# LSTM gates kept in PSUM, and five slots for gathered rows, in a graph network's LSTM

## What is computed

```python
seq = x[col].reshape(n, deg, d)            # 6250 nodes, 17 steps, 128
def step(carry, x_t):
    h, c = carry
    gates = x_t @ w_ih.T + h @ w_hh.T + b
    i, f, g, o = jnp.split(gates, 4, axis=-1)
    c = sigmoid(f) * c + sigmoid(i) * tanh(g)
    h = sigmoid(o) * tanh(c)
    return ((h, c), None)
```

## Time and profile before

| | us |
|---|---|
| median of 3 runs (2754.47 to 2767.64) | 2761.33 |
| the profiled execution | 2727.64 |
| its span | 2725.8 |

### The profile page before, as it was taken

One profiled execution on the slowest core, in us unless ns is written; L12 is line 12 of the kernel. 1 busy time (PEld: TensorE's weight loads), 2 busy tenths in 40 slices (PEclk: granted clock), 3 DMA queues, 4 the chain that ended last, 5 costly groups with the idle time before them and its releaser, 6 DMA issues. The chain is left out here.

```text
span 2725.8 us, 31186 instructions
## 1 busy us (share of the span) xinstructions
PE 2091.4 (77%) x10250; PEld 1626.9 (60%) x10250; DVE 1669.4 (61%) x4013; ACT 1030.3 (38%) x2257; POOL 1805.5 (66%) x1672
## 2 busy tenths in 40 slices
PE   6588888888888888888677677766776676767866
PEld 5477777767677777777545455544554444544545
DVE  4455655655566666665657556665675665656767
ACT  3455555555555555555422222222222222222321
POOL 1667777677777777775366667766777677767660
PEclk8789989989999989998878779877888788878889
DMA  8666766566666666665211111111111111111111
GB/s 303 203 188 205 209 184 183 165 179 178 179 182 178 180 177 182 177 177 145 85 43 42 47 47 44 47 42 43 47 50 44 42 46 47 46 43 45 40 42 48
DMA packets 120893, 310.32 MB, mean 114 GB/s; under 512 B 29042, under 2 KB 42460, under 8 KB 120604
## 3 DMA queue, kind: packets, MB, share of 16 engines
q0 software_dynamic: 93264, 273.00, 35.5%
q1 hardware_dynamic: 27468, 35.33, 3.8%
HBM read 288.95 MB, written 19.26 MB: 113 GB/s over the span
## 5 line engine op out<-in xcount | busy, mean ns | idle before, releaser
L645 POOL DMA_INDIRECT sender<-table,src_index x832 | 899.3, 1081 | 444.7 <-issue 285.1
L372 POOL DMA_INDIRECT shared<-gates,seq_index x833 | 895.2, 1075 | 383.3 <-issue 236.2
L426 ACT ACTIVATE shared<-bank,bias 128x512 f32<-128x512 f32 (+1 forms) x884 | 556.1, 664 | 583.7 <-PE bank L402 236.2
L694 PE MATMUL bank<-msg,select 128*128 128x256 f32 x1664 | 500.3, 452 | 277.0 <-DVE msg L789 165.6
L390 PE MATMUL bank<-ident,shared 128*128 128x128 f32 x3332 | 467.2, 293 | 181.4 <-issue 78.4
L694 PEld LDWEIGHTS bank<-msg,select 128*128 128x128 f32 x1664 | 353.2, 223 | 365.0 <-issue 299.0
L390 PEld LDWEIGHTS bank<-ident,shared 128*128 128x128 f32 x3332 | 412.1, 151 | 244.4 <-issue 199.5
L720 ACT ACTIVATE h<-bank,b 128x512 f32<-128x512 f32 x104 | 71.5, 688 | 861.6 <-remote 456.5
L763 DVE TENSOR_TENSOR select<-shared,rel 128x512 f32<-128x512 f32 x208 | 142.3, 684 | 390.6 <-remote 358.8
L402 PE MATMUL bank<-h_hi,w_lo 128*128 128x512 f32 (+1 forms) x832 | 353.1, 424 | 7.4 <-issue 7.0
L681 PEld LDWEIGHTS bank<-a,h 64*128 64x128 f32 x1664 | 217.8, 196 | 209.7 <-issue 204.6
(11 more groups left out here) (90 smaller groups left out, 2037.3 us busy)
## 6 DMA issues: line engine op xcount, KB each, us to landing
shared<-gates,seq_index POOLq DMA_INDIRECT x833
sender<-table,src_index POOLq DMA_INDIRECT x832
gates<-shared SPq DMA_DIRECT2D x49, 256.0 KB, 3.9
feats<-attr_in SPq DMA_DIRECT2D x13, 256.0 KB
x<-x_nodes_in SPq DMA_DIRECT2D x12, 256.0 KB
table<-up SPq DMA_DIRECT2D x12, 256.0 KB, 2.3
out<-x SPq DMA_DIRECT2D x12, 256.0 KB
shared<-x_t_in SPq DMA_DIRECT2D x3, 704.0 KB, 9.7
```

Source lines behind the costliest of these rows:

```text
L372: pool.indirect_dma_start(out=rows[:, k % 4, j, :], out_offset=None, in_=t["gates"], in_offset=bass.IndirectOffsetOnAxis(ap=seq_index[:, c ...
L426: act_e.activation(act[:, k % 2, gate, 0:width], banks[n % 8][:, 0:width], ACT.Tanh if gate == 2 else ACT.Sigmoid, bias=bias2[:, gate:gate ...
L645: pool.indirect_dma_start(out=sender[:, hg % 4, j, :], out_offset=None, in_=t["table"], in_offset=bass.IndirectOffsetOnAxis(ap=src_index[: ...
L694: last = pe.matmul(acc_bank[i % 3][:, 0:MSG], select[:, hg % 2, j, :], msg[:, hg % 2, j].rearrange("p k u -> p (k u)"), start=(tile in FIR ...
```

## The change

ScalarE writes gates i, f and o back into the banks that it reads them from; the candidate g alone goes to SBUF, into `candidate`, two buffers of 512 columns. VectorE's product of i and candidate goes into `candidate`, forget gate by cell and the hidden product are written into their own banks, and the high and low parts of h are taken from the bank of gate o. Tanh of the cell of item k-1 comes ahead of gate f of item k and waits for the hidden product of k-3 instead of the low part. ScalarE's waits for the cell and the low part, and VectorE's last wait of an item, are gone. TensorE waits bank by bank: gate i's for the input product (the cell in step 0) of k-2, gate f's for its cell, gate o's for its low part of h. The rows have five slots. The first block's views of the pool move, with the same sizes.

```diff
-        pool_cols = 4 * 4 * 4 * HID + 8 * CHUNK
+        slot_cols = 4 * 4 * HID
+        pool_cols = SLOTS * slot_cols + 2 * CHUNK
...
                     for k, (step, c) in enumerate(WORK):
-                        if 4 <= k < NCH + 4:
-                            pool.wait_ge(s_gate, 4 * (k - 3))
-                        elif k >= 4:
-                            pool.wait_ge(s_turned, k - 3 - NCH)
+                        if SLOTS <= k < NCH + SLOTS:
+                            pool.wait_ge(s_gate, 4 * (k - SLOTS + 1))
+                        elif k >= SLOTS:
+                            pool.wait_ge(s_turned, k - SLOTS + 1 - NCH)
...
-                        if k >= 2:
-                            pe.wait_ge(s_act, 4 * (k - 1))
                         for q, gate in enumerate(GATES):
                             bank, cols = banks[4 * (k % 2) + q], slice(gate * HID, (gate + 1) * HID)
+                            if k >= 2 and q == 0:
+                                if k - 2 < NCH:
+                                    pe.wait_ge(s_cell, k - 1)
+                                else:
+                                    pe.wait_ge(s_ig, k - 1 - NCH)
+                            if k >= 2 and q == 2:
+                                if k - 2 < NCH:
+                                    pe.wait_ge(s_act, 4 * (k - 2) + 3)
+                                else:
+                                    pe.wait_ge(s_cell, k - 1)
+                            if k >= 2 and q == 3:
+                                pe.wait_ge(s_hidden, k - 1)
...
-                            act_e.wait_ge(s_hidden, k - 1)
+                            act_e.wait_ge(s_new, k - 1)
                         act_e.activation(tanh_c[:, k % 2, 0:width], cell[:, c0:c0 + width],
...
-                            if q == 0 and k >= 2:
-                                act_e.wait_ge(s_cell, k - 1)
-                            if q == 3 and k >= 2:
-                                act_e.wait_ge(s_hidden, k - 1)
+                            if q == 2 and k:
+                                tanh_cell(k - 1)
+                            values = banks[n % 8][:, 0:width]
                             act_e.wait_ge(s_gate, n + 1)
-                            act_e.activation(act[:, k % 2, gate, 0:width], banks[n % 8][:, 0:width],
+                            act_e.activation(candidate[:, k % 2, 0:width] if gate == 2 else values, values,
...
-                        if k:
-                            tanh_cell(k - 1)
...
-                        dve.tensor_tensor(o, o, tanh_c[:, k % 2, 0:width], ALU.mult).then_inc(s_new, 1)
+                        dve.tensor_tensor(out, out, tanh_c[:, k % 2, 0:CHUNKS[WORK[k][1]][1]], ALU.mult).then_inc(s_new, 1)
...
-                        dve.tensor_copy(h_hi[:, c0:c0 + width], act[:, k % 2, 3, 0:width]).then_inc(s_hi, 1)
+                        dve.tensor_copy(h_hi[:, c0:c0 + width], banks[4 * (k % 2) + 3][:, 0:width]).then_inc(s_hi, 1)
...
-                        dve.tensor_tensor(h_lo[:, c0:c0 + width], act[:, k % 2, 3, 0:width],
+                        dve.tensor_tensor(h_lo[:, c0:c0 + width], banks[4 * (k % 2) + 3][:, 0:width],
                                           h_hi[:, c0:c0 + width].bitcast(F32), ALU.subtract).then_inc(s_hidden, 1)
...
-                            dve.tensor_tensor(gates[:, 0], gates[:, 0], gates[:, 2], ALU.mult).then_inc(s_ig, 1)
+                            dve.tensor_tensor(added, put, added, ALU.mult).then_inc(s_ig, 1)
...
-                            dve.tensor_tensor(gates[:, 1], gates[:, 1], here, ALU.mult).then_inc(s_fc, 1)
+                            dve.tensor_tensor(keep, keep, here, ALU.mult).then_inc(s_fc, 1)
...
-                            dve.tensor_tensor(here, gates[:, 0], gates[:, 1], ALU.add).then_inc(s_cell, 1)
+                            dve.tensor_tensor(here, keep, added, ALU.add).then_inc(s_cell, 1)
...
-                        dve.wait_ge(s_act, 4 * k + 4)
```

More of the change, by code:

```diff
@@ L32 @@
 GATES = (0, 2, 1, 3)
+SLOTS = 5
 GROUP = 8
@@ L118, in build @@
         s_const = sem("s_const")
-        s_wait = [sem(f"s_gather{i}") for i in range(4)]
+        s_wait = [sem(f"s_gather{i}") for i in range(SLOTS)]
         def flat_view(tile):
@@ L177, in build @@
             pool_of = shared[:, NODE_COLS:NODE_COLS + pool_cols]
-            rows_cols = 4 * 4 * 4 * HID
-            rows = pool_of[:, 0:rows_cols].rearrange("p (s j n) -> p s j n", s=4, j=4)
-            act = pool_of[:, rows_cols:rows_cols + 8 * CHUNK].rearrange("p (s g n) -> p s g n", s=2, g=4)
+            rows = pool_of[:, 0:SLOTS * slot_cols].rearrange("p (s j n) -> p s j n", s=SLOTS, j=4)
+            candidate = pool_of[:, SLOTS * slot_cols:pool_cols].rearrange("p (s n) -> p s n", s=2)
             x_t = cell
-            in_rows = rows.rearrange("p s j n -> p (s j) n")
-            w_ih = act[:, 0, 0, :]
-            inside, inside2 = (act[:, 1].rearrange("p g n -> p (g n)")[:, i:i + EDGE_TILES] for i in (0, 1024))
+            in_rows = pool_of[:, 0:8 * CHUNK].rearrange("p (s n) -> p s n", s=8)
+            w_ih, inside, inside2 = (pool_of[:, (8 + i) * CHUNK:(8 + i) * CHUNK + cols]
+                                     for i, cols in ((0, CHUNK), (1, EDGE_TILES), (3, EDGE_TILES)))
             seq_index = sb("seq_index", [P, NODE_TILES * STEPS], I32, scope=scope)
@@ L372, in _ @@
                             pool.indirect_dma_start(
-                                out=rows[:, k % 4, j, :], out_offset=None, in_=t["gates"],
+                                out=rows[:, k % SLOTS, j, :], out_offset=None, in_=t["gates"],
                                 in_offset=bass.IndirectOffsetOnAxis(ap=seq_index[:, col:col + 1], axis=0),
-                            ).then_inc(s_wait[k % 4], 16)
+                            ).then_inc(s_wait[k % SLOTS], 16)
                 @block.tensor
                 def _(pe):
-                    landed = [0] * 4
+                    landed = [0] * SLOTS
                     pe.wait_ge(s_idx, 64)
@@ L382, in _ @@
                         c0, width = CHUNKS[c]
-                        landed[k % 4] += 16 * (width // P)
-                        pe.wait_ge(s_wait[k % 4], landed[k % 4])
-                        if k >= 2:
-                            pe.wait_ge(s_act, 4 * (k - 1))
+                        landed[k % SLOTS] += 16 * (width // P)
+                        pe.wait_ge(s_wait[k % SLOTS], landed[k % SLOTS])
                         for q, gate in enumerate(GATES):
                             bank, cols = banks[4 * (k % 2) + q], slice(gate * HID, (gate + 1) * HID)
+                            if k >= 2 and q == 0:
[10 more added lines that the diff above has]
+                                pe.wait_ge(s_hidden, k - 1)
                             for j in range(width // P):
-                                last = pe.matmul(bank[:, j * P:(j + 1) * P], rows[:, k % 4, j, cols], ident[:],
+                                last = pe.matmul(bank[:, j * P:(j + 1) * P], rows[:, k % SLOTS, j, cols], ident[:],
                                                  is_transpose=True, start=(j == 0), stop=False,
@@ L437, in hidden_product @@
                     def hidden_product(k):
-                        width = CHUNKS[WORK[k][1]][1]
+                        out = banks[4 * (k % 2) + 3][:, 0:CHUNKS[WORK[k][1]][1]]
                         dve.wait_ge(s_tanh, k + 1)
-                        o = act[:, k % 2, 3, 0:width]
-                        dve.tensor_tensor(o, o, tanh_c[:, k % 2, 0:width], ALU.mult).then_inc(s_new, 1)
+                        dve.tensor_tensor(out, out, tanh_c[:, k % 2, 0:CHUNKS[WORK[k][1]][1]], ALU.mult).then_inc(s_new, 1)
                     def hidden_hi(k):
@@ L459, in _ @@
                         here = cell[:, c0:c0 + width]
-                        gates = act[:, k % 2, :, 0:width]
+                        put, keep = banks[4 * (k % 2)][:, 0:width], banks[4 * (k % 2) + 2][:, 0:width]
+                        added = candidate[:, k % 2, 0:width]
                         n = k - NCH + 1
@@ L463, in _ @@
                         if step == 0:
-                            dve.tensor_tensor(here, gates[:, 0], gates[:, 2], ALU.mult).then_inc(s_cell, 1)
+                            dve.tensor_tensor(here, put, added, ALU.mult).then_inc(s_cell, 1)
                         else:
-                            dve.tensor_tensor(gates[:, 0], gates[:, 0], gates[:, 2], ALU.mult).then_inc(s_ig, 1)
+                            dve.tensor_tensor(added, put, added, ALU.mult).then_inc(s_ig, 1)
                         if k:
```

## The result

| | before, us | after, us |
|---|---|---|
| median (4 runs each) | 2757.9 | 2928.6 |
| lowest to highest | 2752.34 to 2767.64 | 2920.24 to 2933.78 |
| profiled execution | 2727.64 | 2933.78 |
| mean granted TensorE clock in it | 0.861 | 0.884 |

After takes 1.0612 times as long as before [1.0569, 1.0655]: 171 us more by the medians. The forecast was 303 us more.

What follows compares the result with a forecast made beforehand. GpSimd's gathers were taken to fill 67.7 of 72.6 us an LSTM step. Hold 172 + clock 70 + slow instructions 60 - step 0's 3 = +299 us on 2727.6: 3027, or 3064 at the median; range 2910 to 3190.

Steps and rivals of the forecast that it cites:

- The hold of gate o's bank: LSTM steps 1 to 16: TensorE waits at gate o for h_lo of k-2; 6.70 us a chunk against 4.50, +172 us.
- The chain: LSTM, gate g's matmuls, tanh g, VectorE's operations up to h_lo, then TensorE's last transposes: 6.70 us between first matmuls.
- The clock: TensorE in LSTM steps 1 to 16: granted clock 0.88, 24% of the time at the lower level, +70 us (0 to +110).
- Slow instructions: TensorE in LSTM steps 1 to 16: before's stalls ahead of transposes, 68.5 us, stay; +60 us (0 to +110).
- the ring: LSTM steps 1 to 16: the round through TensorE, ScalarE and VectorE that sets the chunk period, 6.70 us at full clock.
- Step 0: First LSTM step, no matmuls: a gather a slot earlier and 0.1 us shorter, 70.4 to about 67, -3 us (-9 to +3).
- PSUM operands: LSTM, VectorE and ScalarE: PSUM forms take the SBUF forms' times, pitch 0.60 us, only h_hi's pitch rising from 0.47.
- Tanh moved ahead: ScalarE in the LSTM: taking tanh of the cell ahead of sigmoid f is worth nothing in steps 1 to 16.
- Five slots: LSTM gathers: a fifth slot lets a gather be issued a chunk earlier, worth nothing in steps 1 to 16.
- Rival 1: LSTM steps 1 to 16: gathers were the bound and the hold is hidden; -102 us, 2659 us, chance 6%.
- Rival 3: TensorE in the LSTM: regular standing keeps it at the lower clock, 8.5 us a chunk; +500 us, 3260 us, chance 9%.
- the other 16 us: Each LSTM step of before beyond TensorE's 56.2 us: gathers not landed, stretches at half clock, TensorE's instructions coming slowly.

Runs made afterwards that it cites:

- e1: After with VectorE finishing product, high and low part of item k-1 before item k, and ScalarE's cell tanh ahead of gate i: 2720.25 us, 1.0009 of before.
- e2: After with the hidden product in an SBUF tile, TensorE's gate-o wait ending with that product: 2729.33 us, 1.0046 of before.
- e3: Before with one added wait, TensorE for the low part of k-2 ahead of gate o's transposes of k: 3215.7 us.
- e8: After with tanh of the cell of k-1 behind gate o of k, as in before: 3313.26 us.
- e7: After with four slots instead of five: 2899.82 us, 1.0649 of before.
- e5: Before with each gather replaced by a plain DMA of the same 256 KB from SyncE, rows side by side, GpSimd silent: 2414.87 us.
- e6: Before with gathers for even items only from step 1 on: 2459.68 us.

## Why the prediction was right, and where its sizes were off

The direction, the cause and the place were right, and the time lay in the range, near its lower end: of the 303 us forecast 171 came, because two terms that were guessed and not worked out (clock and slow instructions) were far too large. By its steps:

- **The hold of gate o's bank.** Forecast 6.70 us a chunk, 83.4 a step, 1334 us in all. Measured 6.54 at full clock (687.54 to 694.08, the first matmuls of two chunks), a mean of 6.58, and 83.9 a step, 1343 us in all. The three periods around the 128-node chunk are about 6.2, 4.7 and 5.4 instead of 6.4, 4.4 and 5.6. The chain was right link by link; the gap from h_lo to TensorE is 0.06 instead of 0.10, and tanh g's end to VectorE 0.02 (645.79 + 0.69 to 646.50) instead of 0.10. e1 and e2 shorten the hold and the loss is gone; e3 adds it alone and loses more.
- **The clock, +70 us, mis-sized.** I took 0.88 and measured 0.97, higher than before's 0.91. I had argued from shares of standing time. After stands 28% (373.6 of 1343.0) and has 0.97; the edge stage, also 28%, has 0.83; e3 and e8 stand 35% (572.1 of 1647.4, 614.3 of 1736.0) and have 0.91 and 0.87. The share alone does not tell the clock.
- **Slow instructions, +60 us, mis-sized.** I carried before's stalls over as something that the new slack cannot hide. As far as the runs show they go with GpSimd's unbroken issuing, which the hold itself breaks: they all but vanished, as ScalarE's waits show in after and e3. Clock and slow instructions together are what lies between 1343 and the ring at full clock. That is 10 x 6.54, 6.22 into and about 4.7 out of the 128-node chunk and 5.4 behind it, 81.7 us a step or 1308 us: 35 us in place of 130, most of them in the first three periods of a step. These 95 us and the 26 by which the ring is shorter than 1334 are the 121 us by which the stage came in under the forecast (1464 against 1343).
- **Step 0, -3 us, wrong in sign: +9.** Without matmuls I saw only the earlier gather. But the new waits run through ScalarE and VectorE there too, and a late signal now hits TensorE:

```profile
91.72 1.40 ACT L436 ACTIVATE bank<-bank,bias 128x512 f32<-128x512 f32 x2 [6.34 <-remote]
...
94.64 0.69 DVE L472 TENSOR_TENSOR shared<-bank,shared 128x512 f32<-128x512 f32 x1 [13.50 <-ACT shared L436]
...
97.44 2.82 PE L401 MATMUL bank<-ident,shared 128*128 128x128 f32 x12 [10.88 <-DVE h_lo L458]
```

- **PSUM operands.** Right: sigmoid bank to bank 0.66 us, VectorE's forms 0.68 to 0.69, pitch 0.60, the CAST from a bank 0.68 where from SBUF it took 0.55.
- **Tanh moved ahead, "worth nothing" in steps 1 to 16.** Wrong: 1.3 us a chunk (e8), 393 us in the profiled runs of this stage (1736.0 against 1343.0), the lower clock included. The working of the ring already had tanh in its early place, so the sum was not touched, but the sentence was. What an edit is worth has to be asked of the path that the other edits leave.
- **Five slots worth nothing.** Right (e7).
- **Rival 1, the gathers as the bound.** I gave it 102 us if the hold were hidden. e1 and e2 hide most of it and have the faster gathers (the sum of gathers and issue falls from 1060 to 940 us), and gain nothing: the stage stays some 200 us above that sum, with 160 us of GpSimd's idle time put down to late signals. e1's own ring and e2's remaining waits take part in this, so the rival is not tested cleanly; what they show is that faster gathers alone do not bring the 102 us.
- **Rival 3, the lower clock.** It did not come: the clock was 0.97. The time that I gave for a clock of 0.7, 3160 us, does not follow from my terms: with 194 us for the clock in place of 70 they give about 3190 us at the median, and about 3130 without the slow instructions.
- **What I called "the other 16 us" of a step** of before was a list of three symptoms, gathers not landed, half clock, slow instructions. e5 removes all three by taking GpSimd's gathers away, and with them 1162.4 - 893.0 = 269 us, GpSimd's own pace included. I had the rows and did not see what they have in common.

The profiled execution of after came in 93 us under the 3027 of the sum: 121 less in steps 1 to 16, 12 more in step 0, 17 more behind the LSTM and half a microsecond in the first block. The other 42 of the 135 us by which the median lies under 3064 come from the step from the profiled run to the median: I raised the sum by the ratio of before's median to its profiled run, and after's profiled run (2933.78) is the slowest of its four, not the fastest.

## What to carry to other kernels

If a bank or buffer that was freed right behind its first reader is kept for a result that an in-order engine makes last in its next round, cost the whole round from the first gate that it needs, link by link; here that gave the new period within 3%. Don't carry the stalls of the old kernel over into the new one as a sum of their own before their cause is known, since the change may remove it. And a gather engine that looks full may not be all that the kernel waits for: shortening its gathers by an eighth brought nothing here (e1, e2), taking them away 269 us. Replace its transfers by plain ones of the same size before its relief is priced.

## What the runs showed of the hardware that was not expected

- Gathers issued by GpSimd without a rest go with TensorE's signals arriving 4 to 5 us late at ScalarE and GpSimd (e1) and with TensorE's instructions coming slowly (before). Plain loads from SyncE at 235 GB/s show neither (e5), nor do half as many gathers (e6). Whether it is the missing rest or the rate of gathers is open.
- Two SBUF operands on VectorE slow a gather beside them not always: 1081 ns in before, 970 in e3 with the same operations, 1104 in e6, against 948 in after.
- Standing 28% of the time, TensorE had a granted clock of 0.97 in after's LSTM and of 0.83 in before's edge stage; standing 35%, 0.91 in e3 and 0.87 in e8.
